# A post-norm transformer stack by groups of sequences: first group's start by sequences, last group's end by halves, six norms' outputs on ScalarE

## What is computed

```
x = layernorm(x + attention(x))     # v, q = x @ vq_w.T ; k = sigmoid(x @ key_w.T + key_b)
                                    # per head (16 of 8): state_t = k_t * state_{t-1} + (1 - k_t) * v_t (outer)
                                    # h = q . state ; h @ out_w.T + out_b
x = layernorm(x + x @ W[i] + b[i])  # i: one of 8 experts, an argmax over logits and noise
x = layernorm(x + metric(x))        # per head: P = x proj ; (P M)(P^T P) ; @ mixer_w.T + mixer_b
x = layernorm(x + mlp(x))           # silu(x w1)*(x w2), two hidden layers of 512 with gelu, then w3
```

## Time and profile before

| | us |
|---|---|
| median of 3 runs (204.56 to 205.01) | 204.92 |
| the profiled execution | 203.15 |
| its span, first to last instruction | 201.4 |
| PE busy | 177.6 (88%) |
| DVE busy | 149.0 (74%) |
| ACT busy | 117.4 (58%) |
| POOL busy | 68.4 (34%) |

### The profile page before, as it was taken

One profiled execution on the slowest core, in us unless ns is written; L12 is line 12 of the kernel. 1 busy time (PEld: TensorE's weight loads), 2 busy tenths in 40 slices (PEclk: granted clock), 3 DMA queues, 4 the chain that ended last, 5 costly groups with the idle time before them and its releaser, 6 DMA issues.

```text
span 201.4 us, 2831 instructions
## 1 busy us (share of the span) xinstructions
PE 177.6 (88%) x940; PEld 137.7 (68%) x940; DVE 149.0 (74%) x388; ACT 117.4 (58%) x178; POOL 68.4 (34%) x60
## 2 busy tenths in 40 slices
PE   7886878788976999999999999999899899999930
PEld 7245566466864887998789889866678677586810
DVE  0299999999999999999999955756772255753143
ACT  2698544095501785525577753498786459975720
POOL 4020002402012335343705545152549670554401
PEclk9999999999999999999999999999999999999995
DMA  5995002100000000010000000000001010000101
GB/s 144 333 433 215 3 0 80 52 0 0 3 0 0 3 3 0 0 52 3 0 2 0 3 0 0 0 0 3 0 0 37 19 52 3 2 0 1 51 3 55
DMA packets 6273, 7.83 MB, mean 39 GB/s; under 512 B 497, under 2 KB 5105, under 8 KB 6001
## 3 DMA queue, kind: packets, MB, share of 16 engines
q1 hardware_dynamic: 6256, 7.63, 11.1%
HBM read 6.58 MB, written 1.05 MB: 38 GB/s over the span
## 4 chain that ended last, share of the span: by engine, by line
PE 54%; DVE 23%; issue 10%; ACT 7%; DMA 2%; POOL 2%; POOLq 1%; DVEq 0%; SPq 0%; ACTq 0%
PE c_bank L1199 30%; DVE state L731 8%; PE y_bank L1106 7%; PE b_bank L1134 4%; PE b_bank L1129 3%; DVE read L741 3%; DMA heads_pack<-heads 2%; DVE stats L774 2%; PE rep_bank L1094 2%; PE b_bank L1199 2%; PE sum_bank L1199 2%; PE b_bank L1160 1%; DVE normed_lent L759 1%; DVE normed_lent L801 1%; ACT hid_even_high L482 1%
## 5 line engine op out<-in xcount | busy, mean ns | idle before, releaser
L731 DVE TENSOR_TENSOR_SCAN state<-rep_bank,keep 128x256 f32<-128x256 f32 x64 | 40.4, 675 | 2.3 <-PE rep_bank L1094 2.1
L1106 PEld LDWEIGHTS y_bank<-attend_pack,read 128*128 128x128 f32 x256 | 31.9, 191 | 8.2 <-DVE read L741 4.7
L1106 PE MATMUL y_bank<-attend_pack,read 128*128 128x128 f32 x256 | 33.6, 277 | 3.2 <-DVE total L766 1.9
L292 POOL TENSOR_TENSOR rstd<-varied,power 128x4 f32<-128x4 f32 x16 | 18.5, 1158 | 42.9 <-DVE varied L788 42.8
L741 DVE TENSOR_TENSOR read<-state,query 128x512 f32<-128x512 f32 x32 | 23.0, 730 | 0.5
L301 POOL TENSOR_TENSOR hid_odd_low<-hid,hid_odd_high 128x512 fp32r<-128x512 f32 x12 | 16.3, 1364 | 16.7 <-ACT hid L493 16.7
L493 ACT ACTIVATE hid<-c_bank,scales_pack 128x512 f32<-128x512 f32 x32 | 21.6, 683 | 0.0
L487 ACT ACTIVATE hid_even_high<-c_bank,scales_pack 128x512 fp32r<-128x512 f32 x16 | 11.0, 688 | 17.5 <-PE c_bank L1199 17.3
L1199 PE MATMUL c_bank<-hid_even_high,hidden_rounded 128*128 128x512 f32 x64 | 19.4, 410 | 1.0 <-ACT hid_even_high L482 0.8
L1199 PE MATMUL c_bank<-hid_odd_high,hidden_rounded 128*128 128x512 f32 x64 | 19.1, 410 | 0.0
L1199 PE MATMUL c_bank<-hid_odd_low,hidden_rounded 128*128 128x512 f32 x64 | 18.5, 398 | 0.4 <-DVE hid_odd_low L835 0.4
(11 more groups left out here) (133 smaller groups left out, 336.6 us busy)
## 6 DMA issues: line engine op xcount, KB each, us to landing
hidden_pack<-hidden SPq DMA_DIRECT2D x2, 1024.0 KB, 11.0
xT_lent<-x_chan SPq DMA_DIRECT2D x4, 256.0 KB, 5.7
xt<-x_tok SPq DMA_DIRECT2D x4, 256.0 KB, 2.8
mlp_pack<-mlp SPq DMA_DIRECT2D x1, 768.0 KB, 8.0
out<-xT_lent SPq DMA_DIRECT2D x3, 256.0 KB, 2.3
attend_pack<-attend SPq DMA_DIRECT2D x1, 640.0 KB, 5.1
metric_pack<-metric SPq DMA_DIRECT2D x1, 448.0 KB, 12.5
out<-xT_lent SPq DMA_DIRECT2D x2, 128.0 KB, 1.8
```

Source lines behind the costliest of these rows:

```text
L292: nc.gpsimd.tensor_tensor(rstd[n][:], varied[n][:], power[:], ALU.pow).then_inc(ln_rstd[n], 1)
L731: ins = nc.vector.tensor_tensor_scan(state[:, e % STATES, at], rep_bank[e % 2][:, at], keep[:, a * T + s * SEQ:a * T + (s + 1) * SEQ], 0.0 ...
L1106: ins = nc.tensor.matmul(y1_bank[:, tile(j)], read[:, e % READS, tile(j)], out_w_rep_sb[:, e, :], start=(e == 0 and j == 0), stop=False, s ...
```

## The change

- **Packs and loads.** `project` becomes `values` and `keys` (with the query's weights), `heads` becomes `rows` and `sums`. The first group's x is loaded a sequence at a time. Order: values, sequence 0, keys, sequence 1, rows, scales, sums, attend, the rest as before.
- **First group up to its first scan.** Values and keys are projected by sequence into four banks, the query into `y1_bank`; copies, steps, highs, lows, `replicate` and `scan` of step 0 are done for 256 columns at a time. `cast_rows` casts first what the steps 0 and 1 need. The memset of `value` covers only its first column. Six warm-up calls instead of eight.
- **Norms 0, 1, 2 of groups 0 and 1.** DVE computes shift = -mean * rstd (`norm_shift`), and ACT writes x * rstd + shift in four `Identity` activations with scale and bias from SBUF. Groups 2 and 3, and norm 3, stay on DVE.
- **The last group's end.** Of the second hidden layer's last quarter on, gelus, low part, `narrow`, `narrow_out`, `turn_back`, the sum, statistics, power and `norm_out` are done by halves of 256 columns. The second half uses other banks.
- **Orders.** The lists of all four engines are rewritten. Ahead of the branch PE now also has `replicate(2, 4)`, `replicate(2, 5)`, `attend(2, 1)` and `attend(2, 2)`; the metric step and `transposes(b, 2)` of later groups stand earlier among the hidden layers. `silu_table(2)` and `silu_table(3)` stand beside the silus.

```diff
-WARM_UP = 8
+WARM_UP = 6
...
-    ("project", (("key_w", P), ("value_w", P), ("query_w", P), ("key_b", 1))),
-    ("heads", (("rows_of", HD * HEADS), ("head_sum", P))),
+    ("values", (("value_w", P),)),
+    ("keys", (("key_w", P), ("query_w", P), ("key_b", 1))),
+    ("rows", (("rows_of", HD * HEADS),)),
+    ("sums", (("head_sum", P),)),
...
-            load_pack("project")
-            for g in range(NG):
+            load_pack("values")
+            sp.dma_start(xT[:, 0:SEQ], x_chan[:, 0:SEQ]).then_inc(x0_loaded, 16)
+            load_pack("keys")
+            sp.dma_start(xT[:, SEQ:T], x_chan[:, SEQ:T]).then_inc(xT_loaded[0], 16)
+            load_pack("rows")
+            load_pack("scales")
+            load_pack("sums")
+            load_pack("attend")
+            for g in range(1, NG):
                 at = slice(g * T, (g + 1) * T)
                 sp.dma_start(xT[:, at], x_chan[:, at]).then_inc(xT_loaded[g], 16)
-                if g == 0:
-                    load_pack("heads")
-                    load_pack("scales")
-                    load_pack("attend")
             load_tokens(0)
...
+                nc.gpsimd.memset(value[:, :, 0:1], 0.0).then_inc(const_ready, 1)
...
+            def inverse_std_last(i):
+                pool.wait_ge(last["varied"], i + 1)
+                at = slice(i * NT // 2, (i + 1) * NT // 2)
+                nc.gpsimd.tensor_tensor(rstd[3][:, at], varied[3][:, at], power[:, at], ALU.pow).then_inc(last["rstd"], 1)
...
+            def cast_rows(i):
+                n = (0, 2, HD)[i], (0, 2, HD)[i + 1]
+                act.wait_ge(loaded["rows"], 16)
+                nc.scalar.copy(rep_r[:, n[0]:n[1], :].rearrange("p e (h d) -> p e h d", h=HEADS),
+                               rows_of_sb[:, n[0]:n[1], :].unsqueeze(3).to_broadcast([P, n[1] - n[0], HEADS, HD])
+                               ).then_inc(rep_cast, 1)
...
+            def norm_out(n, g):
+
+                act.wait_ge(ln_shift[n], g + 1)
+                if g > 0:
+
+                    act.wait_ge(turned[n], g)
+                    if n == 2:
+                        act.wait_ge(res_ready[3], g)
+                for j in range(NT):
+                    nc.scalar.activation(normed[n][:, tile(j)], total[n][:, tile(j)], ACT.Identity,
+                                         bias=shift[n][:, j:j + 1], scale=rstd[n][:, j:j + 1]).then_inc(ln_out[n], 1)
...
+            def first_value(s):
+                act.wait_ge(first["proj"], 2 * s + 1)
+                act.wait_ge(const_ready, 3)
+                nc.scalar.copy(value[:, s, 1:SEQ + 1], proj_bank[s][:, 0:SEQ]).then_inc(first["out"], 1)
...
+            def first_keep(s):
+                act.wait_ge(first["proj"], 2 * s + 2)
+                act.wait_ge(loaded["keys"], 16)
+                nc.scalar.activation(keep[:, s * SEQ:(s + 1) * SEQ], (b4_bank, b5_bank)[s][:, 0:SEQ], ACT.Sigmoid,
+                                     bias=key_b_sb).then_inc(first["out"], 1)
...
+            def first_high(s):
+                act.wait_ge(*((first["steps"], 1), (dv_whole, 1))[s])
+                nc.scalar.copy(dvalue_parts[0][0][half(0), s * SEQ:(s + 1) * SEQ],
+                               dvalue[half(0), s * SEQ:(s + 1) * SEQ]).then_inc((first["high"], dv_high)[s], 1)
...
+            def high_gelu_last(i):
+                act.wait_ge(hidden_ready, 2 * NH * NG)
+                at = slice(i * T // 2, (i + 1) * T // 2)
+                nc.scalar.activation(hid_parts[2][0][:, NH - 1, at], c_bank[1][:, at], ACT.Gelu,
+                                     scale=h2s_sb[:, NH - 1:NH]).then_inc(last["gelu_high"], 1)
...
             sigmoid_table()
-            cast_rows()
-            projected(0)
-            projected(1)
-            high_values(0, 0)
+            cast_rows(0)
+            first_value(0)
+            first_keep(0)
+            first_value(1)
+            first_high(0)
+            first_high(1)
             high_values(0, 1)
-            projected(2)
+            first_keep(1)
+            first_query()
+            cast_rows(1)
             projected(3)
             routing(0)
             routing(1)
             projected(4)
+            routing(2)
+            round_weights(0)
...
+            norm_out(2, 0)
             high_x3(0)
             silu(0, 0)
             silu(0, 1)
+            norm_out(0, 1)
+            move_x1(1)
             silu(0, 2)
+            high_values(3, 0)
             high_product(0, 0)
-            high_values(3, 0)
-            move_x1(1)
-            keep_residual(0)
+            silu(0, 3)
             high_product(0, 1)
...
+            def first_steps(s):
+                dve.wait_ge(first["out"], 2 * s + 1)
+                nc.vector.tensor_tensor(dvalue[:, s * SEQ:(s + 1) * SEQ], value[:, s, 0:SEQ], value[:, s, 1:SEQ + 1],
+                                        ALU.subtract).then_inc((first["steps"], dv_whole)[s], 1)
+
+            def first_low(s):
+                dve.wait_ge(*((first["high"], 1), (dv_high, 1))[s])
+                at, parts = slice(s * SEQ, (s + 1) * SEQ), dvalue_parts[0][0]
+                nc.vector.tensor_tensor(parts[half(1), at], dvalue[half(0), at], parts[half(0), at].bitcast(F32),
+                                        ALU.subtract).then_inc((first["low"], dv_ready)[s], 1)
+
+            def first_scan(s):
+                dve.wait_ge(*((first["rep"], 1), (rep_ready, 1))[s])
+                dve.wait_ge(first["out"], 2 * s + 2)
+                at = slice(s * SEQ, (s + 1) * SEQ)
+                nc.vector.tensor_tensor_scan(state[:, 0, at], (sum_bank, rep_bank[0])[s][:, at], keep[:, at], 0.0, ALU.add,
+                                             ALU.mult).then_inc((first["scan"], scan_done)[s], 1)
...
+            def norm_shift(n, g):
+                dve.wait_ge(ln_rstd[n], g + 1)
+                if g > 0:
+                    dve.wait_ge(ln_out[n], NT * g)
+                nc.vector.scalar_tensor_tensor(shift[n][:], moments[n][:, :, 0], -1.0, rstd[n][:], ALU.mult,
+                                               ALU.mult).then_inc(ln_shift[n], 1)
...
+            def norm_out_last(i):
+                dve.wait_ge(last["rstd"], i + 1)
+                dve.wait_ge(stored, 16 * (NG - 1))
+                for j in range(i * NT // 2, (i + 1) * NT // 2):
+                    nc.vector.tensor_scalar(normed[3][:, tile(j)], total[3][:, tile(j)], moments[3][:, j, 0:1],
+                                            rstd[3][:, j:j + 1], ALU.subtract, ALU.mult).then_inc(ln_out[3], 1)
+
...
+            first_steps(0)
             top_logit()
             shifted_logits()
-            value_steps(0)
-            low_values(0, 0)
+            first_steps(1)
+            first_low(0)
+            first_low(1)
+            first_scan(0)
+            first_scan(1)
             low_values(0, 1)
-            scan(0, 0)
             read_state(0, 0)
             scan(0, 1)
+            scan(0, 2)
             read_state(0, 1)
+            scan(0, 3)
+            read_state(0, 2)
             direct_product(0)
             value_steps(1)
-            scan(0, 2)
-            read_state(0, 2)
...
+            direct_product(2)
+            norm_shift(2, 0)
+            read_state(2, 2)
+            scan(2, 3)
             norm_stats(0, 1)
-            norm_out(2, 0)
-            rounding_flag()
-            scan(2, 1)
+            norm_moments(0, 1)
             low_x3(0)
...
+            low_gelu_last(0)
+            low_gelu_last(1)
+            norm_sum_last(0)
+            norm_stats_last(0)
+            norm_moments_last(0)
+            norm_varied_last(0)
+            norm_sum_last(1)
+            norm_stats_last(1)
+            norm_moments_last(1)
+            norm_varied_last(1)
+            norm_out_last(0)
+            norm_out_last(1)
...
+            def first_replicate(s):
+                pe.wait_ge(*((first["low"], 1), (dv_ready, 1))[s])
+                pe.wait_ge(rep_cast, 1)
+                at = slice(s * SEQ, (s + 1) * SEQ)
+                nc.tensor.matmul((sum_bank, rep_bank[0])[s][:, at], rep_r[:, 0, :], dvalue_parts[0][0][:, at], start=True,
+                                 stop=True).then_inc((first["rep"], rep_ready)[s], 1)
...
+            def narrow_early(i):
+
+                if i == 0:
+                    pe.wait_ge(gelu_done, 2 * NH * NG - 1)
+                else:
+                    pe.wait_ge(scan_done, HD * NG)
+                bank_, at = (c_bank[0], rep_bank[0])[i], slice(i * T // 2, (i + 1) * T // 2)
+                for n in range(2):
+                    for k in range(NH - 1):
+                        if n == 0:
+                            pe.wait_ge(gelu_high, 2 * NH * (NG - 1) + NH + k + 1)
+                        else:
+                            pe.wait_ge(*low_done(NG - 1, 2, k))
+                        x = hid_parts[2][n][:, k, at]
+                        nc.tensor.matmul(bank_[:, 0:T // 2], w3_forms[exact[0]][:, k, :],
```

(51 more changed lines are left out.)

588 lines of the change are left out of this document (326 added, 262 removed).

## The result

The changed kernel took 198.84 us (median of 4 runs, 198.54 to 200.12), the kernel before 204.96 (204.56 to 205.15) beside it: ratio 0.9716, 95% interval 0.9671 to 0.9761. It is faster by 6.1 us; the forecast was 200.3. Its profiled execution took 198.95 us with a span of 197.2, against 203.15 and 201.4: 4.2 us less, where the working gave 4.65.

A forecast was written before the change was run, and what follows sets the result against it. DVE bounds up to the gate, PE after it, then a chain of single operations. Gains 1.0 + 2.25 + 0.1 + 1.3 = 4.65 us take the profiled 203.15 to 198.5, median 200.3; range 197.7 to 203.4.

The forecast's parts named there:

- The head: Start to first read_state: pack lands at 5.5 us, read starts at 10.1 against 12.40, 2.3 us earlier.
- "+0.3" for the stream: DVE's operations from first read_state up to the gate: added scans, reads and shifts against fewer norm operations, 0.3 us more.
- "+0.7" for stalls: DVE waits before the gate because norms through ACT take longer: 0.7 us more, bounds 0 and 2.5.
- a sign of being wrong: Before the gate: DVE idling before norm_sum(1, 0) and mask_gram(0) would show the prediction wrong; no size given.
- "+0.3" at the gate: Entry to the MLP: the norm's wait splits the first pair of gate matmuls, 0.3 us more.
- PE's work and gaps: From the gate on: 2.25 us less PE work, moved ahead of the gate, and 0.1 us less idle (+0.8, -0.9).
- The end: Last hidden layer's first gelu to last norm_out, by halves: 1.3 us gained, bounds 0.8 and 2.0.
- with the same offset 200.3: Whole kernel: median stays 1.77 us above the profiled execution as before, so 198.5 becomes 200.3.
- lost in the norms: Rival: three norms before the gate wait for ACT, 2.5 us instead of 0.7, MLP gaps grow; 202.6 us, chance 0.20.
- blocked nothing behind the gate: Rival: in-order ACT norm outputs hold up silus or gelus in the MLP; 208.1 us for three, chance 0.10.
- the pack wasn't late: Rival: in the head, rows lands at 7.0 us and only 0.8 is gained; 201.8 us, chance 0.12.
- more than I count: Rival: no stalls, other PE gaps close, power goes by columns, pack lands by 4.8; 197.9 us, chance 0.18.

The follow-up runs named there:

- e5: Changed kernel with two POOL calls swapped in group 1, passed_weights ahead of attend_residual(1); median 198.37 us, ratio 0.972.
- e11: Changed kernel with passed_weights ahead of attend_residual(1) on POOL and eight idle PE matmuls between flag_sum and through_metric(0); median 197.13 us, ratio 0.966.
- e12: Changed kernel with passed_weights ahead of attend_residual(1) on POOL and eight idle PE matmuls behind the last turn_back_last(1); median 197.20 us, ratio 0.968.
- e2: Changed kernel with the last group's end whole again instead of by halves; median 199.70 us, ratio 0.978.
- e3: Changed kernel with all six ACT norm outputs back on DVE, in place of the shifts; median 202.93 us, ratio 0.994.

## Why the prediction was right, and where it wasn't

**The head** gained 1.71 us for 2.3 (in the eleven other profiles with the new head the read is at 9.92 to 10.81). The pack was 0.4 early. The walk behind it was almost 1.0 us too short (5.52 us from the cast to the read for 4.55). I let the second `value` follow ACT's copies without pause, and it waited for PE: it was out 1.94 us behind the cast's start, where I had 1.30. The rest, 0.3, is small change in the scans and the low behind it.

The Trainium skill ("DMA: Bandwidth & Descriptors", Anatomy of one DMA) would have had the pack at 4.8, an estimate; its rule is fitted to transfers that GpSimd issues, and SP issued this one. The trace has it at 5.1, 0.3 later.

**DVE's stream and its stalls** were counted at +1.3 us with the gate's entry. The change had 0.36: DVE's busy time fell by 1.34 us (51.10 to 49.76), and its idle time grew by 1.70 (1.15 to 2.85). Without a dip, and with e5's swap on POOL (e11, e12), the stretch is 1.6 shorter than before, 50.65 for 52.25:

```profile
10.81:61.46 50.65, 45.26 (x267) 33.37 (x265) 50.01 (x121) 31.80 (x50) 6.04 (x6) 1.00 0.22 84
```

So three steps failed there. "+0.3" for the stream: DVE's busy time from read to gate is 49.76 (50.01 in e12) for 51.10, 1.1 to 1.3 less. By lines it has 38 scan instructions for 34 and 19 reads for 18, three shifts and none of the twelve `norm_out` instructions; I had counted to the last `replicate`, by which two reads more and one `norm_stats` less came in, where the stretch to the gate itself has one read more and as many statistics. "+0.7" for stalls: they grew by 1.7 in the changed kernel, and DVE idled at both places that the prediction had named as a sign of being wrong; with the wait for POOL gone and the clock up, it idles 0.6 us in all of the stretch. "+0.3" at the gate: the norm's longer way is there, ACT's four instructions take 1.65 us (I had 1.5), but varied to gate fell from 5.2 to 4.63, for the branch's 0.63 no longer stood ahead of the first matmul. What stood against these gains was a thing that the prediction had left out: the granted clock. Its trace had 1.00 everywhere before the end, and I took that for a property of the kernel. Over the profiles of the new order the stretch takes 50.6 us without a dip (both with e5's swap), 51.5 to 52.6 with one of 3.4 us, and 54 to 55.3 with a long one or two. e5 and e12 have the same streams up to the gate and take 54.89 us with a dip of 10.3 us and 50.65 with none: 4.2 us, nearly the whole gain that I worked out.

The Trainium skill ("ScalarE: Activation LUTs", What ACT_TABLE_LOAD costs) gave 1.64 us for the four instructions, an estimate; the trace agrees, at 482 ns each and 1.65 us for four.

**PE's work and gaps** were right: 2.59 us for 2.35, of which PE's busy time is 2.55 (123.08 to 120.53; I had 2.25), and its idle time is 2.69 for 2.73. The pieces were as walked: 0.64 us of idle behind the gate where there was none (+0.8 forecast), and the gap of 0.86 between 150 and 166 us is gone (-0.9); the last window has 0.38 more.

**The end** gained 1.60 us to the norm, for 1.3, and lost 1.34 behind it. The forecast ended with the last `norm_out` and took the 2.29 behind it as fixed. e2 shows the loss is with the halves, e12 that it is not of the halves' making: they bring the stores forward into the instruction transfer. The step that failed is that I took what lies behind the last operation as a constant.

**From sum to median.** The sum missed its profiled execution by 0.45 us. That it came so close is luck in part, for larger misses cancel in it: -0.6 in the head, +0.9 up to the gate, +0.2 to the gelu, +0.3 to the norm, -1.3 behind it. It missed the median by 1.46: the step "with the same offset 200.3" was off. The profiled execution before was 1.8 us under its median, the one after is 0.1 over. In later runs of the kernel before, the clock mostly reads 0.985 to 0.990 where the span is 201 to 202, 0.978 to 0.982 where it is 202.4 to 202.8, and 0.962 to 0.973 where it is 203 to 206. So its profile showed an undisturbed run (0.989), and its median did not. The 3.4 us of one dip at half the clock would take 0.008 off the mean, an estimate, about what lies between the first two groups. That dips are what lengthens the others is argued from those pairs; no trace of such a run was there.

**The rivals.** The lead wasn't lost in the norms, ACT blocked nothing behind the gate (PE waits there 0.2 us at a time) and has no more table loads than before (12 for 14), and the pack wasn't late. e3 turns the blocked ACT round: with the norms on DVE, PE idles 2.4 us more in the MLP. The rival "more than I count" gave 197.9, and the median of 198.84 is nearer to it than to my 200.3. Its reasons didn't come true, though: the stalls were there, PE's idle time behind the gate stayed at 2.69 us, and the pack came at 5.1; only the power was shorter than I took it, 0.7 for 0.8. That the median lies near its number comes from the offset.

Two smaller readings were off too. PE reads 9 until the last two slices of the page before, not three. And the runs tell this kernel from no change by 0.45% to either side, the interval's half width, not by 0.2%.
